# Attention weights loaded and split earlier, projections a block ahead, and gate logits with the tokens on the partitions

## What is computed

```python
h = tok(x, conv_w, conv_b, pos_table)            # patches @ conv_w + conv_b + pos_emb
h = concatenate([cls_tok, h])
q, k, v = (n @ A @ W for A, W in ((qA, qB), (kA, kB), (vA, vB)))   # layer 0: n = layernorm(h), rank 48
q, k = q * cos + rot(q) * sin, k * cos + rot(k) * sin              # 6 heads of 32, causal softmax
h = h + softmax(mask(q @ k.T / sqrt(32))) @ v @ o_w
gates = softmax(n @ gate_w + gate_b)                               # 32 experts, every token in each
h = h + sum_e gates[e] * (gelu(n @ w1[e] + b1[e]) @ w2[e] + b2[e])
h = h + relative_attention(n)    # layer 1: 12 heads of 64, tables for keys and values; then top 1 of 8 experts
h = h + performer_attention(n)   # layer 2: then a block of attention, MLP and 4 experts with top-2 gates
h = h + quantised_attention(n)   # layer 3: then a block with routed attention and an MLP
```

## Time and profile before

| | |
|---|---|
| median of three runs | 3219.13 us (3214.16 to 3223.34) |
| the profiled execution | 3218.63 us |
| its span | 3216.8 us |
| mean granted clock of TensorE | 0.936 |
| PE busy | 2892.5 us (90%), 19899 matmuls |
| PE weight loads | 2674.1 us (83%) |
| DVE busy | 2116.5 us (66%) |
| ACT busy | 1099.7 us (34%) |
| POOL busy | 640.0 us (20%) |
| DMA | 105.58 MB, mean 33 GB/s |

### The profile page before, as it was taken

How to read it: one execution, slowest core, us unless ns; L and a number is a source line. 1 busy time by engine, 2 the same in 40 slices (tenths; PEclk the granted TensorE clock), 3 DMA queues, 4 the chain that set the end, 5 groups by cost and what they waited for, 6 DMA issues and landing times. The chain is left out here.

```text
span 3216.8 us, 56579 instructions
## 1 busy us (share of the span) xinstructions
PE 2892.5 (90%) x19899; PEld 2674.1 (83%) x19899; DVE 2116.5 (66%) x5306; ACT 1099.7 (34%) x2247; POOL 640.0 (20%) x764
## 2 busy tenths in 40 slices
PE   6879999999999999999996998896979889876877
PEld 5769999999999999999986887674768779766767
DVE  2757777777767777777775765234467657787776
ACT  2443333233333333333333333213445333334433
POOL 1211121212212122121212100112223112122440
PEclk8979999999999999999998999798989879988888
DMA  3010100000000000000000000560000000000000
GB/s 131 1 52 18 35 35 35 29 23 35 35 35 19 33 35 35 35 18 35 18 37 1 2 2 5 156 203 30 1 11 19 35 18 18 11 1 15 23 18 17
DMA packets 23889, 105.58 MB, mean 33 GB/s; under 512 B 4391, under 2 KB 9399, under 8 KB 18382
## 3 DMA queue, kind: packets, MB, share of 16 engines
q1 hardware_dynamic: 22078, 99.62, 8.9%
q0 software_dynamic: 1584, 3.30, 0.3%
HBM read 98.32 MB, written 6.64 MB: 33 GB/s over the span
## 5 line engine op out<-in xcount | busy, mean ns | idle before, releaser
L792 ACT ACTIVATE hid<-bank,dat 128x384 f32<-128x384 f32 (+1 forms) x912 | 554.5, 608 | 1154.3 <-PE bank L510 1058.6
L761 PE MATMUL bank<-w,hid_hi 128*128 128x384 f32 x2964 | 848.7, 358 | 0.0
L763 PE MATMUL bank<-w,hid_lo 128*128 128x192 f32 x2964 | 742.0, 250 | 0.0
L763 PEld LDWEIGHTS bank<-w,hid_lo 128*128 128x128 f32 x2964 | 565.8, 191 | 1.4
L824 DVE TENSOR_TENSOR hid_lo<-hid,hid_hi 128x384 fp32r<-128x384 f32 (+1 forms) x912 | 539.9, 592 | 31.6
L761 PEld LDWEIGHTS bank<-w,hid_hi 128*128 128x128 f32 x2964 | 556.4, 188 | 1.6
L821 DVE CAST hid_hi<-hid 128x384 fp32r<-128x384 f32 (+1 forms) x912 | 341.2, 374 | 148.2 <-ACT hid L792 147.5
L510 PE MATMUL bank<-xa_hi,w_hi 128*128 128x384 f32 (+1 forms) x912 | 327.9, 360 | 9.8 <-DVEq L2123 5.5
L835 DVE SCALAR_TENSOR_TENSOR h_tok<-bank,gate,h_tok 128x192 f32<-128x192 f32 x416 | 173.4, 417 | 245.6 <-PE bank L763 240.6
L510 PE MATMUL bank<-xb,w_hi 128*128 128x384 f32 (+1 forms) x912 | 326.5, 358 | 0.0
L510 PE MATMUL bank<-xb,w_lo 128*128 128x384 f32 (+1 forms) x912 | 326.1, 358 | 0.0
(11 more groups left out here) (347 smaller groups left out, 4538.0 us busy)
## 6 DMA issues: line engine op xcount, KB each, us to landing
raw<-in_L_exp SPq DMA_DIRECT2D x36, 1344.0 KB, 5.6
w_e<-in_L_exp SPq DMA_DIRECT2D x20, 576.0 KB, 4.0
w_e<-in_L_exp SPq DMA_DIRECT2D x20, 384.0 KB
pix<-in_pixels SPq DMA_DIRECT2D x6, 832.0 KB, 11.0
w_e<-in_L_exp SPq DMA_DIRECT2D x20, 195.0 KB
wp_raw<-in_L_att SPq DMA_DIRECT2D x1, 2880.0 KB, 9.6
raw<-in_L_mlp SPq DMA_DIRECT2D x2, 1344.0 KB, 5.7
route_rows<-in_rows_clear SPq DMA_DIRECT2D x1, 2000.0 KB, 20.7
```

Source lines behind the costliest of these rows:

```text
L761: nc.tensor.matmul(o[:, 0:2 * D], hid_hi[k % 2][:, m, c], w2[j][:, m, :], start=m == 0, stop=False)
L763: ins = nc.tensor.matmul(o[:, 0:D], hid_lo[k % 2][:, m, c], w2[j][:, m, 0:D], start=False, stop=m == HC - 1)
L792: nc.scalar.activation(hid[(6 * k + m) % 3][:, 0:128 * nt], bank[4 + (6 * k + m) % 4][:, 0:128 * nt], func, bias=bias).then_inc(s["h_act"] ...
```

## The change

- **Factors.** `low` is the first transfer of the program. TensorE makes the ten factor products before the convolution, in banks 3 to 7, and ScalarE copies each pair into `wp_raw` in one instruction. The convolution waits for a bank where it first writes it. A pad keeps `wp_raw` clear of what the convolution reads. The output weights are loaded behind the constants.
- **First attention's weights.** `attention_weights(l0, 1, alone=True)`: GpSimd makes the cast and the subtraction, beside the features.
- **Relative attention's weights.** The query, key and value weights are loaded when the last expert's weights have been split, cast and subtracted on GpSimd during the features. The output weights are loaded after the last expert into a part of `o_f`, and cast and subtracted by GpSimd after the attention's first two stagings; TensorE waits for them at the first output projection, ScalarE at its first copy that overwrites their buffer.
- **Causal order.** The projections of a block come one slot earlier; VectorE signals each rotation done, and ScalarE waits for that one of the block before instead of for the whole block. `keep_clock` makes 8 products instead of 11.
- **Gate logits** of the first and the third layer: tokens on the partitions, three matmuls for each tile with the high and low gate weights side by side, a bias product for each group of tiles, and VectorE adds the two halves as it reads the bank (`tensor_reduce`).
- **Turned gates.** Four groups of transposes instead of 13 single ones, in the first expert before the second quarter; the products with the second biases come behind the second quarter's `up`. In the routed second layer both stand where the old ones stood.

The diff, cut to what matters:

```diff
+                pe.wait_ge(factors["in"], 16)
+                for m in range(5):
+                    f = (0, 0, 1, 1, 2)[m]
+                    for k in range(2):
+                        ins = nc.tensor.matmul(bank[3 + m][:, D * k:D * k + D],
+                                               low[:, 256 * f + 128 * k:256 * f + 128 * k + 128],
+                                               low[:, 768 + D * m:768 + D * m + D], start=True, stop=True)
+                    ins.then_inc(factors["full"], 1)
...
+                        if c == 0 and t >= 3:
+                            pe.wait_ge(factors["moved"], t - 2)
                         product(t, c)
...
+            def scalar(act):
+                products = wp_raw[:, 0:10 * D].rearrange("p (k c) -> p k c", k=2)
+                for m in range(5):
+                    act.wait_ge(factors["full"], m + 1)
+                    nc.scalar.activation(products[:, :, D * m:D * m + D],
+                                         bank[3 + m][:, 0:2 * D].rearrange("p (k n) -> p k n", k=2), ACT.Identity)\
+                        .then_inc(factors["moved"], 1)
+            phases.append(dict(tensor=tensor, vector=vector, scalar=scalar))
...
+        TURNED = [(0, 4), (4, 4), (8, 4), (12, 1)]
...
+            PER = TILES if plain else min(TILES, 512 // (2 * E))
+            groups = [(t0, min(PER, TILES - t0)) for t0 in range(0, TILES, PER)]
...
-                NJ = TOK // 4
-                for j in range(4):
-                    c = slice(NJ * j, NJ * (j + 1))
-                    five(bank[j][0:E, 0:NJ], [gw_hi[:, 0, 0:E], gw_hi[:, 1, 0:E]],
-                         [gw_lo[:, 0, 0:E], gw_lo[:, 1, 0:E]], xa_hi[:, c], xa_lo[:, c], xb[:, c], True)\
-                        .then_inc(s["job_full"].sem, 1)
...
+                for k, (t0, nt) in enumerate(groups):
+                    o = bank[k][:, 0:2 * E * nt].rearrange("p (t e) -> p t e", t=nt)
+                    nc.tensor.matmul(o, row[0:1, ROW_COLS["ones"]],
+                                     row[0:1, ROW_COLS[gb_col]].unsqueeze(1).to_broadcast([1, nt, 2 * E]),
+                                     start=True, stop=False)
+                    for t in range(t0, t0 + nt):
+                        c, last = slice(128 * t, 128 * t + 128), t == t0 + nt - 1
+                        nc.tensor.matmul(o[:, t - t0, :], xa_hi[:, c], gw[:, 0, 0:2 * E], start=False, stop=False)
+                        nc.tensor.matmul(o[:, t - t0, 0:E], xa_lo[:, c], gw[:, 0, 0:E], start=False, stop=False)
+                        ins = nc.tensor.matmul(o[:, t - t0, :], xb[:, c], gw[:, 1, 0:2 * E], start=False, stop=last)
                 ins.then_inc(s["job_full"].sem, 1)
             def turn(pe):
-                pe.wait_ge(s["job_full"].sem, b["job_full"] + logits_done + 1)
...
-                pe.wait_ge(s["t_used"].sem, b["t_used"] + TILES)
+                pe.wait_ge(s["job_full"].sem, b["job_full"] + 2)
+                for q, (t0, nt) in enumerate(TURNED):
+                    if q == 3:
+                        pe.wait_ge(s["t_used"].sem, b["t_used"] + 1)
+                    for t in range(t0, t0 + nt):
+                        ins = nc.tensor.transpose(bank[1 + q % 3][0:E, 128 * (t - t0):128 * (t - t0) + 128], gate[:, t, 0:E],
+                                                  shp[:, SHAPE_COLS["ident"]])
+                    ins.then_inc(s["t_full"].sem, 1)
+            def turned(pe):
+                pe.wait_ge(s["t_used"].sem, b["t_used"] + len(TURNED))
...
             def keep_turned(act):
...
+                for q, (t0, nt) in enumerate(TURNED):
+                    act.wait_ge(s["t_full"].sem, b["t_full"] + q + 1)
+                    nc.scalar.activation(gate_t[0:E, 128 * t0:128 * (t0 + nt)], bank[1 + q % 3][0:E, 0:128 * nt],
                                          ACT.Identity).then_inc(s["t_used"].sem, 1)
...
-                dve.wait_ge(s["job_full"].sem, b["job_full"] + logits_done)
-                lg = bank[0][:, 0:TILES * E].rearrange("p (t e) -> p t e", e=E)
-                link(nc.vector.tensor_copy(v3(3), lg))
+                    link(nc.vector.tensor_copy(gw[:, :, 0:E], w))
+                    link(nc.vector.tensor_tensor(gw[:, :, E:2 * E], w, gw[:, :, 0:E].bitcast(F32), ALU.subtract))
+                dve.wait_ge(s["job_full"].sem, b["job_full"] + 1)
+                if plain:
+                    ins = nc.vector.tensor_copy(v3(3), bank[0][:, 0:TILES * E].rearrange("p (t e) -> p t e", e=E))
+                else:
+                    for k, (t0, nt) in enumerate(groups):
+                        both = bank[k][:, 0:2 * E * nt].rearrange("p (t u e) -> p t e u", u=2, e=E)
+                        ins = nc.vector.tensor_reduce(v3(3)[:, t0:t0 + nt, :], both, AX.X, ALU.add)
+                link(ins)
...
                 def second_biases():
                     if gating:
-                        gating["tensor"][1](pe)
+                        gating["tensor"][2](pe)
...
-                    if is_first(e):
-                        second_biases()
+                    if is_first(e) and gating:
+                        gating["tensor"][1](pe)
                     for k in range(1, 4):
                         up(e, j, k)
+                        if is_first(e) and k == 1:
+                            second_biases()
                         down(e, j, k - 1)
...
                     split(e, j, 0)
-                    if is_first(e):
-                        add_second_biases()
                     for k in range(1, 4):
                         split(e, j, k)
+                        if is_first(e) and k == 1:
+                            add_second_biases()
                         gather(e, j, k - 1)
...
             def sync(sp):
+                if low_rank:
+                    return
                 sp.wait_ge(s["phase_done"].sem, 3 * after)
+                sp.dma_start(wp_raw[:, 0:cols], a[cfg.dram]).then_inc(s["att_in"].sem, 16)
+            def weights_in(eng):
                 if low_rank:
-                    sp.dma_start(low[:, :], a[cfg.dram + "_low"]).then_inc(s["att_in"].sem, 16)
-                    sp.dma_start(wp_raw[:, 2 * cfg.C:cols], a[cfg.dram]).then_inc(s["att_in"].sem, 16)
+                    eng.wait_ge(factors["moved"], 5)
+                    eng.wait_ge(factors["out_in"], 16)
                 else:
-                    sp.dma_start(wp_raw[:, 0:cols], a[cfg.dram]).then_inc(s["att_in"].sem, 16)
+                    eng.wait_ge(s["att_in"].sem, b["att_in"] + 16)
...
+                weights_in(act)
...
                 if alone:
-                    pool.wait_ge(s["att_in"].sem, b["att_in"] + 16)
+                    weights_in(pool)
                     nc.gpsimd.tensor_copy(wp_hi[:, 0:cols], wp_raw[:, 0:cols]).then_inc(s["att_hi"].sem, 1)
...
+        def relative_weights(cfg, after):
+            QKV, OUT = 2 * cfg.C, cfg.no * D
+            b = base(att_ready=1)
+            free = signals["w_split"].at
+            def sync(sp):
+                sp.wait_ge(s["w_split"].sem, free)
+                sp.dma_start(wp_raw[:, 0:QKV], a[cfg.dram][:, 0:QKV]).then_inc(wide_in["qkv"], 16)
+                sp.wait_ge(s["phase_done"].sem, 3 * after)
+                sp.dma_start(out_raw, a[cfg.dram][:, QKV:QKV + OUT]).then_inc(wide_in["out"], 16)
+            def gpsimd(pool):
+                pool.wait_ge(wide_in["qkv"], 16)
+                nc.gpsimd.tensor_copy(wp_hi[:, 0:QKV], wp_raw[:, 0:QKV]).then_inc(wide_in["high"], 1)
+                for m in [xs[:, p, :, :].rearrange("p j (m s) -> p (j m) s", s=32)[:, :, SLOT:32] for p in range(3)] \
+                        + [p[:, :, SLOT:32] for p in p_t] + [v_x[:, :], rel_a[:, :, 20:32]]:
+                    nc.gpsimd.memset(m.bitcast(F32) if m.dtype == F32R else m, 0.0)
+                pool.wait_ge(wide_in["high"], 1)
+                nc.gpsimd.tensor_tensor(wp_lo[:, 0:QKV], wp_raw[:, 0:QKV], wp_hi[:, 0:QKV].bitcast(F32),
+                                        ALU.subtract).then_inc(wide_in["low"], 1)
+                pool.wait_ge(wide_in["low"], 1)
+                n = 4 * cfg.G * SLOT
+                nc.gpsimd.memset(q_t[:, 0:cfg.no_q * (n + 8)].rearrange("p (c n) -> p c n", n=n + 8)[:, :, n:n + 8],
+                                 0.0).then_inc(s["att_ready"].sem, 1)
+            return dict(sync=sync, gpsimd=gpsimd)
+        def output_weights(pool, cfg):
+            c = slice(2 * cfg.C, 2 * cfg.C + cfg.no * D)
+            pool.wait_ge(wide_in["out"], 16)
+            nc.gpsimd.tensor_copy(wp_hi[:, c], out_raw).then_inc(wide_in["out_high"], 1)
+            pool.wait_ge(wide_in["out_high"], 1)
+            nc.gpsimd.tensor_tensor(wp_lo[:, c], out_raw, wp_hi[:, c].bitcast(F32), ALU.subtract)\
+                .then_inc(wide_in["out_ready"], 1)
+            pool.wait_ge(wide_in["out_ready"], 1)
...
-                    order = [("exp", 2, 0), ("bd", 1, 0), ("values", 0, 0), ("v", 2, 0), ("scores", 3, 0), ("qk3", 0, 1),
```

(33 more changed lines are left out.)

80 lines of the change are left out of this document (17 added, 63 removed).

## The result

| | before | changed |
|---|---|---|
| median, same chip, five runs each | 3214.97 us (3212.73 to 3223.34) | 3200.74 us (3199.16 to 3205.19) |
| ratio, with its 95% interval | | 0.995 (0.9939 to 0.9962) |
| the changed kernel in a further set (e1) | 3215.71 us | 3198.27 us (3190.53 to 3204.43), 0.9942 (0.9925 to 0.9959) |
| profiled execution, span | 3218.63, 3216.8 us | 3200.74, 3198.9 us |
| mean granted clock of TensorE | 0.936 | 0.936 |

A forecast was written before the change was run, and what follows sets the result against it. TensorE is never idle in the first layer's expert loop, so gains were sought in the gaps between stages. Eight terms summed to -36.6 us against 3218.63, giving 3182.0 us, with a range of 3167 to 3197.

The forecast's parts named there:

- Term 1: Factor products ahead of the convolution: start 2.6 us later, 3.1 given back, so -0.5 us; bounds +2.6 to -1.5.
- Term 2: First attention's weights: POOL's work beside the features brings ScalarE's first copy to 69.5 from 76.10, -6.6 us.
- Term 3: Causal attention, projections a block ahead: VectorE's three waits for k_t go, -4.5 us; fewer clock-keeping products counted as nothing.
- rival of ScalarE's new wait: First attention: ScalarE stalls at twelve waits for rotations, 72 us at 6 us each, giving 3258 us; chance 0.03.
- Terms 4 and 7: Gate logits, first and third layer: 39 small products at the low level, -1.9 and -7.8 us.
- rival of the high level: Gate logits, first and third layer: stages run at the high level, 10 us more gained, 3172 us; chance 0.13.
- Terms 5 and 8: Turned gates and second biases, first and third layer: -6.6 us each; gain 4.4 if TensorE is at the low level.
- Term 6: Relative attention's weights loaded early, POOL's work beside the features holding VectorE: -2.1 us; output weights 0, up to +2.
- Half-gains: Waits return elsewhere (+4.5), both bias stretches run low (+4.4), convolution gives nothing back (+3.1): 3194 us; chance 0.15.

The follow-up runs named there:

- e2: Changed kernel with the factor products moved behind the convolution, to the head of the features stage, and `low` loaded behind the constants; 3192.89 us, 0.993.
- e3: Changed kernel with POOL waiting for VectorE's last scale before cast and subtraction of the first and relative attention's weights; 3187.31 us, 0.9906.
- e13: Kernel before the change with 8 clock-keeping products instead of 11; 3214.06 us, one execution.
- e7: Changed kernel with the projections back in their old places in the causal order, new waits and eight clock-keeping products kept; 3200.16 us, 0.9945.
- e6: Kernel before the change, run again unchanged for a second trace; 3221.19 us, one execution.
- e9: Kernel before the change with only the pad added, which moves the convolution's row of biases in SBUF; 3214.24 us, one execution.
- e14: Changed kernel with 11 clock-keeping products instead of 8; 3200.42 us, one execution.
- e4: Changed kernel with the second biases in front of the second quarter again, grouped gate transposes kept; 3193.61 us, 0.9929.
- e5: Changed kernel with the relative attention's weights loaded, cast and subtracted as before the change; 3201.24 us, 0.9952.
- e11: Changed kernel with cast and subtraction of the relative attention's output weights moved behind GpSimd's second block copy; 3202.93 us, one execution.

## Why the prediction was wrong, and where it was right

- **Term 1, mis-sized.** The failed step is "the factor products pay for the low level that the convolution paid for". The start comes 2.9 us later (11.48 against 8.59), and the first 96 matmuls give back 1.3 and not 3.1: +1.6, within the bounds of the term, and +2.5 in e1. The other 1.7 (3.3 in e1) come with the fall of the clock, which kernels without the early products have too; for that the term had no bound. The low level lasts 3.2 to 5.9 us of the convolution with the factor products in front and 3.5 to 6.1 without, so they don't pay it. e2 gets 2.6 back.
- **Term 2, right, with its mechanism.** Forecast (L467 is L492 now): L467 meets the subtraction and ends with it at 54.5; it ended at 57.66 in a stage that began 3.3 later. e3 shows the hold itself.
- **Term 3, half of what it gave.** The failed step is "ten projection matmuls now stand in front of them and the scores come when they did": the scores come 1.7 us earlier, and the dropped products alone give 2.1 (e13). The order gave 5.9 in the stretch where its waits held 4.5, with the granted clock up from 0.92 to 0.96. That the term gave 4.6 more than forecast is luck, and hides as much of what the others missed. The rival of ScalarE's new wait didn't occur: e7 has the wait and takes no longer than e13 without it.
- **Terms 4 and 7, right.** The 39 products ran 0.21 apart, at the low level; the stages took 11.8 and 9.0 us where I had 11.2 and 8.7. The rival of the high level didn't happen. How close term 4 came is in part luck: the old stage took 13.1 us in the trace that I had, and 16.0 to 16.1 in e6, e9 and e13, where the granted clock was 0.63 in it against 0.78.
- **Terms 5 and 8, mis-sized,** -6.6 against -2.2 and -2.3 to -4.1 (-5.3 for term 5 in e14). I stopped the sum at the first `down` product, where it held (27.28 to 21.99 us, -5.3; 28.20 to 24.12). The failed step is what comes behind: I took the `down` products at the high level, and they run low for some 6 us, +3.1 until the next `up` (5.10 to 8.19). So even the 4.4 that term 8 called the least wasn't reached in either trace of the changed kernel. e4 shows the low stretch wherever the biases stand. I also missed that the two MLPs without gates go through the same code; that came to nothing.
- **Term 6, right** in size (e5) and mechanism, though it was the second L450 and not L467 that met the subtraction (9.55 us). Left out was the attention behind it, +4.4: I had reasons only for the output weights (0, up to +2), and e5 and e11 show that they aren't it. That part is located but not explained.
- **The rivals.** "Half-gains", 3194, was the nearest: its bias stretches and its convolution came true and more (8.7 us for its 4.4, 3.8 for its 3.1), its waits did not. I had given it 0.15 and cut its outer half from the range. The measured time lies 3.7 us above the range and 6.7 above that rival; no rival had the relative attention's 4.4.

## What to carry to other kernels

Count a stage until the next one runs at its old pace, not until its first product: a stretch of small matmuls leaves the granted clock low for the wide ones behind it, and moving it moves the low stretch along. Work given to POOL "beside" VectorE costs VectorE's small operations POOL's whole instruction, so let POOL start when these are done (e3, 11 us by two waits) or cut its instructions (the pieces of the cast let VectorE in, those of a memset not always). And small products put in front of the first big stage don't take the low pace at its start upon themselves: in the changed kernel's two traces they put it off by 2.8 and 2.9 us and gave back 0.4 and 1.3.

## What the runs showed of the hardware

- At its start the convolution runs at half of its later pace (a matmul of 192 columns every 0.32 us, then every 0.16). The change comes 3.2 to 6.1 us behind its first matmul in sixteen traces, whether or not 6.76 us of smaller products (48 x 192) run in front. The clock column shows 1.00 there only because the traces have no record before the change.
- VectorE's operations on 2 to 4 elements get in between the pieces of a POOL cast (0.17 us), and between the eight pieces of a memset in one place (0.33 us) but not in another (3.63 us).
- TensorE can stand 0.5 to 1.05 us in a run of like matmuls with no wait in the profile. In the relative attention ten traces of changed kernels have such stands, and the one with six more matmuls far ahead (e14) has none.
